# Low halves of the weights taken from PSUM, the last weight rows split a tile later, and twice as many table rows fetched by ScalarE

## The reference

```python
e = jnp.stack([tbl_f[ids[:, f]] for f in range(27)], axis=1)      # 2048 x 27 x 128, rows of 27 tables
gram = einsum('bfd,bgd->bfg', e, e)[:, upper triangle without diagonal]   # 351 products per example
h = concatenate([e.reshape(2048, 3456), gram, dense_ctx], axis=1)  # 3456 + 351 + 16 = 3823 columns
h = maximum(h @ W_top1 + b_top1, 0)      # 3823 x 512
h = maximum(h @ W_top2 + b_top2, 0)      # 512 x 256
y = h @ W_top3                           # 256 x 1
```

## Time and profile before

| | |
|---|---|
| median of 3 runs | 560.85 us (558.38 to 560.85) |
| the profiled execution | 560.3 us, of which 558.3 us are the span of the trace |
| busy in the span | PE 93%, PEld 88%, DVE 64%, ACT 42%, POOL 72% |
| chain of waits | PE 58%, POOL 27%, issue 9%, DMA 3% |
| gathers of GpSimd | 421, from 2.9 us to 531.0 us |

### The profile page before, as it was taken

One profiled execution on the slowest core, in us unless ns is written; L12 is line 12 of the kernel. 1 busy time (PEld: TensorE's weight loads), 2 busy tenths in 40 slices (PEclk: granted clock), 3 DMA queues, 4 the chain that ended last, 5 costly groups with the idle time before them and its releaser, 6 DMA issues.

```text
span 558.3 us, 10910 instructions
## 1 busy us (share of the span) xinstructions
PE 521.1 (93%) x2626; PEld 488.6 (88%) x2626; DVE 354.7 (64%) x1177; ACT 234.1 (42%) x721; POOL 404.4 (72%) x439
## 2 busy tenths in 40 slices
PE   0593899999999999999999999999999999999998
PEld 0483899999999999999999999999898998999985
DVE  2644675848476675847576575847567484766865
ACT  2643526254352625344252626345262533526251
POOL 6777777777777777777777777777777777777711
PEclk9988899999999999999999999999999999999999
DMA  8777221122111122121221212121211222121200
GB/s 183 231 212 206 56 55 53 54 57 57 55 55 55 54 60 55 54 56 53 58 57 55 55 55 55 56 58 54 55 54 55 58 55 56 53 55 54 56 11 1
DMA packets 26212, 38.05 MB, mean 68 GB/s; under 512 B 13156, under 2 KB 15588, under 8 KB 26148
## 3 DMA queue, kind: packets, MB, share of 16 engines
q0 software_dynamic: 13472, 27.62, 18.0%
q1 hardware_dynamic: 12164, 9.61, 6.5%
q10 hardware_dynamic: 512, 0.13, 0.1%
HBM read 37.31 MB, written 0.01 MB: 67 GB/s over the span
## 4 chain that ended last, share of the span: by engine, by line
PE 58%; POOL 27%; issue 9%; DMA 3%; DVE 1%; ACT 1%; SPq 0%; ACTq 0%; POOLq 0%; DVEq 0%
POOL emb L327 27%; PE ps_acc L387 14%; PE ps_acc L388 12%; PE ps_acc L389 11%; PE ps_gram L412 7%; PE ps_t L358 5%; PE ps_gram L505 2%; PE ps_acc L446 1%; DMA g_buf<-in_b_top 1%; PE ps_acc L447 1%; PE ps_acc L452 1%; PE ps_gram L498 1%; DMA emb<-in_tbl,idx_first 1%; PE ps_gram L441 1%; ACT g_buf L709 1%
## 5 line engine op out<-in xcount | busy, mean ns | idle before, releaser
L327 POOL DMA_INDIRECT emb<-in_tbl,idx x394 | 372.9, 946 | 120.2 <-issue 118.7
L387 PE MATMUL ps_acc<-w_hi,emb_x 128*128 128x512 f32 x432 | 197.3, 457 | 2.7 <-DVE emb_x L807 1.7
L388 PE MATMUL ps_acc<-w_lo,emb_x 128*128 128x512 f32 x432 | 175.3, 406 | 0.0
L847 DVE COPY g_buf<-ps_gram 32x112 f32<-32x112 f32 x480 | 129.8, 270 | 70.7 <-PE ps_gram L412 64.8
L389 PE MATMUL ps_acc<-w_hi,emb_x 128*128 128x512 f32 x432 | 174.4, 404 | 0.0
L644 ACT ACTIVATE emb_x<-ps_t 128x512 fp32r<-128x512 f32 (+1 forms) x111 | 63.5, 584 | 225.8 <-PE ps_t L358 206.5
L700 ACT ACTIVATE g_buf<-ps_gram 32x112 f32<-32x112 f32 x480 | 122.0, 254 | 56.9 <-PE ps_gram L412 51.2
L807 DVE TENSOR_TENSOR emb_x<-ps_t,emb_x 128x512 fp32r<-128x512 f32 (+1 forms) x111 | 72.8, 666 | 104.2 <-ACT emb_x L644 103.6
L387 PEld LDWEIGHTS ps_acc<-w_hi,emb_x 128*128 128x128 f32 x432 | 131.1, 304 | 8.6 <-issue 5.8
L388 PEld LDWEIGHTS ps_acc<-w_lo,emb_x 128*128 128x128 f32 x432 | 134.6, 312 | 0.8
L389 PEld LDWEIGHTS ps_acc<-w_hi,emb_x 128*128 128x128 f32 x432 | 131.9, 305 | 1.1
(11 more groups left out here) (81 smaller groups left out, 251.5 us busy)
## 6 DMA issues: line engine op xcount, KB each, us to landing
ahead<-in_tbl SPq DMA_DIRECT2D x1152, 0.5 KB
g_buf<-in_W_top SPq DMA_DIRECT2D x29, 256.0 KB, 3.6
emb<-in_tbl,idx POOLq DMA_INDIRECT x394, 2.5
beside<-in_tbl ACTq DMA_DIRECT2D x256, 0.5 KB
w<-in_W_top SPq DMA_DIRECT2D x1, 512.0 KB, 9.1
emb<-in_tbl,idx_first POOLq DMA_INDIRECT x27, 4.0
g_buf<-in_W_top SPq DMA_DIRECT2D x1, 222.0 KB
idx<-in_ids SPq DMA_DIRECT2D x1, 216.0 KB, 4.8
```

What stands on the lines that cost most here:

```text
L327: pool.indirect_dma_start(out=emb[:, f * D:(f + 1) * D], out_offset=None, in_=tables[f], in_offset=bass.IndirectOffsetOnAxis(ap=rows, axis ...
L387: pe.matmul(acc, emb_part(0, f), w_hi[:, f, :], start=(f == 0), stop=False)
L388: pe.matmul(acc, emb_part(0, f), w_lo[:, f, :], start=False, stop=False)
L847: last = dve.tensor_copy(target, source)
```

## The change

Three things:

1. **Low parts of weights.** ScalarE copies each chunk twice: to `w_hi`, and unrounded to a PSUM bank (`whole(c)`, the four gram banks in turn). VectorE's subtraction reads that bank in place of the stage buffer. The stage buffer is free when ScalarE's second copy is done (SyncE waits on `s_w_hi`).
2. **The last three chunks** are loaded into `h1`, `h1_t` and `gram` (buffers not yet in use) instead of stage buffers, with semaphores of their own. Both engines split them in tile 1, ScalarE ahead of its part on group 4, VectorE after packing the products of tile 0. The takes of tile 0 no longer wait for them.
3. **ScalarE fetches four sets of rows**: feature 22 of tiles 5, 8, 12 and 15. So GpSimd has 419 gathers. A tile's part is 38 rows. 22 addresses are loaded at group 4 and 16 more in the gram stage, between the takes of units 0 and 2. The row DMAs: 12 ahead of group 4, 3 ahead of group 5 and `take_columns`, 7 ahead of group 6, 1 each ahead of the takes of units 2, 4 and 8, 3 ahead of group 0 of the next tile (at unit 15), 2 ahead of its group 1 and 8 ahead of its group 2. The buffer `beside` keeps its size (two sets, used in turn).

The diff, cut to its core:

```diff
     BESIDE = 22
-    BESIDE_TILES = [8, 15]
+    BESIDE_TILES = [5, 8, 12, 15]
     NB = len(BESIDE_TILES)
-    A_SET = TILES // 2 - 1
-    A_TILE = 19
-    SLOTS = {4: (0, 11), 6: (11, 16), 2: (16, 19)}
-    assert BESIDE == AHEAD - 1 and A_SET * A_TILE >= P > A_SET * A_TILE - 8
+    A_TILE = 38
+    SLOTS = [("g", 4, 12), ("g", 5, 3), ("g", 6, 7), ("k", 2, 1), ("k", 4, 1), ("k", 8, 1), ("k", 15, 3), ("g", 1, 2), ("g", 2, 8)]
+    LOADS = [("g", 4, 22), ("k", 2, 16)]
+    assert sum(count for _, _, count in SLOTS) == sum(part for _, _, part in LOADS) == A_TILE
+    assert BESIDE == AHEAD - 1 and (TILES - 3) * A_TILE < NB * P <= (TILES - 2) * A_TILE
     HALF = H1 // 2
...
+        def whole(c):
+
+            return ps_gram[:, c % (BANKS + 1), :]
+
+        def cols_raw(n):
+
+            return (h1[:, :], h1_t[:, :], gram.rearrange("p a b -> p (a b)")[:, 0:H1])[n]
+
+        def cols_whole(n):
+
+            return ps_gram[:, BANKS - 1 + n % 2, :]
...
-                return beside[:, BESIDE_TILES.index(t), :]
+                return beside[:, BESIDE_TILES.index(t) % BESIDE_KEPT, :]
...
                 if c >= STAGES:
-                    sp.wait_ge(s_w_lo, c - STAGES + 1)
+                    sp.wait_ge(s_w_hi, c - STAGES + 1)
                 sp.dma_start(stage[:, s, :], w_top1[c * P:(c + 1) * P, :]).then_inc(s_w_raw[s], 16)
...
             for n in range(FULL):
-                load_weights(NF + n)
-            c = NF + FULL
-            sp.wait_ge(s_w_lo, c - STAGES + 1)
-            sp.dma_start(stage[0:REST - 1, c % STAGES, :], w_top1[c * P:K1, :]
-            sp.dma_start(stage[REST - 1:REST, c % STAGES, :],
+                sp.dma_start(cols_raw(n), w_top1[(NF + n) * P:(NF + n + 1) * P, :]
+                             ).then_inc(s_w_cols[n], 16)
+            sp.dma_start(cols_raw(FULL)[0:REST - 1, :], w_top1[(NF + FULL) * P:K1, :]
+                         ).then_inc(s_w_cols[FULL], 16)
+            sp.dma_start(cols_raw(FULL)[REST - 1:REST, :], b_top1.rearrange("(o n) -> o n", o=1)
+                         ).then_inc(s_w_cols[FULL], 16)
...
@@ -399,6 +415,7 @@
                     pe.wait_ge(s_emb_lo, NG * t + NG)
                     if t == 0:
                         pe.wait_ge(s_pads, 1)
+                        pe.wait_ge(s_w_lo, NF)
...
                     pe.wait_ge(s_ones, 2)
+                    pe.wait_ge(s_w_lo, NF + NCC)
...
         def _(act):
             def split_weights(c):
                 act.wait_ge(s_w_raw[c % STAGES], 16 * (c // STAGES + 1))
-                act.activation(w_hi[:, c, :], stage[:, c % STAGES, :],
+                act.activation(w_hi[:, c, :], stage[:, c % STAGES, :], ACT.Copy)
+                if c > BANKS:
+                    act.wait_ge(s_w_lo, c - BANKS)
+                act.activation(whole(c), stage[:, c % STAGES, :],
                                ACT.Copy).then_inc(s_w_hi, 1)
 
             def split_column_weights(n):
-                c, k = NF + n, COL_CHUNKS[n][1]
-                act.wait_ge(s_w_raw[c % STAGES], 16 * (c // STAGES + 1 + n // FULL))
-                act.activation(w_cols_hi[0:k, n, :], stage[0:k, c % STAGES, :],
+                k = COL_CHUNKS[n][1]
+                act.wait_ge(s_w_cols[n], 32 if n == FULL else 16)
+                act.activation(w_cols_hi[0:k, n, :], cols_raw(n)[0:k, :], ACT.Copy)
+                if n == 0:
+                    act.wait_ge(s_dve_raw, UNITS // 2)
+                if n >= 2:
+                    act.wait_ge(s_w_lo, NF + n - 1)
+                act.activation(cols_whole(n)[0:k, :], cols_raw(n)[0:k, :],
                                ACT.Copy).then_inc(s_w_hi, 1)
...
                 act.wait_ge(s_gram, UNITS * t + k + 1)
                 if k == 0:
                     if t == 0:
-                        act.wait_ge(s_w_lo, NF + NCC)
+                        act.wait_ge(s_w_lo, NF)
                     else:
                         act.wait_ge(s_turned, t)
...
+            def load_rows(rows, t, kind, number):
+
...
+                part = next(x for x in LOADS if x[0:2] == (kind, number))[2]
+                first = (t - 1) * A_TILE + len(rows)
+                end = min(first + part, NB * P)
+                while first < end:
+                    n, p = divmod(first, P)
+                    count = min(end - first, P - p)
+                    u = BESIDE_TILES[n]
+                    _, loaded = nc.values_load_multi_w_load_instructions(
+                        at_ahead[u:u + 1, P + p:P + p + count],
+                        engines=[mybir.EngineType.Activation],
+                        min_val=0, max_val=(tables[BESIDE].shape[0] - 1) * ROW,
+                        skip_runtime_bounds_check_because="an id is a row of its table")
+                    rows += [(n, p + i, at) for i, at in enumerate(loaded)]
+                    first += count
+
...
+            def fetch_beside(rows, kind, number):
+
+                slot = SLOTS.index(next(x for x in SLOTS if x[:2] == (kind, number)))
+                first = sum(count for _, _, count in SLOTS[:slot])
+                for n, p, at in rows[first:first + SLOTS[slot][2]]:
+                    if p == 0 and n >= BESIDE_KEPT:
+
+                        act.wait_ge(s_pe_t, NG * BESIDE_TILES[n - BESIDE_KEPT] + BESIDE // GF + 1)
+                    row = beside_bytes[bass.ds(at, ROW)]
+                    act.dma_start(beside[p:p + 1, n % BESIDE_KEPT, :].bitcast(u8),
                                   row.rearrange("(o b) -> o b", o=1)).then_inc(s_beside[n], 16)
...
+                    if t == 1 and g == 4:
+                        for n in range(NCC):
+                            split_column_weights(n)
                     if t > 0 and g == 4:
-                        picked = load_rows(t)
-                    if t > 0 and g in (4, 6) or t > 1 and g == 2:
-                        fetch_beside(picked, g)
+                        picked = []
+                        load_rows(picked, t, "g", 4)
+                    if t > 0 and g in (4, 5, 6) or t > 1 and g in (1, 2):
+                        fetch_beside(picked, "g", g)
                     if t > 0 and g == 5:
                         take_columns(t - 1)
...
-                if t == 0:
-                    for n in range(NCC):
-                        split_column_weights(n)
                 for k in ACT_UNITS:
+                    if t > 0 and k in (2, 4, 8, 15):
+                        if k == 2:
+                            load_rows(picked, t, "k", k)
+                        fetch_beside(picked, "k", k)
                     if k == UNITS - 1:
                         split_group(t + 1, 0)
                     take_blocks(t, k)
...
             def split_weights(c):
                 dve.wait_ge(s_w_hi, c + 1)
-                dve.tensor_tensor(w_lo[:, c, :], stage[:, c % STAGES, :],
+                dve.tensor_tensor(w_lo[:, c, :], whole(c),
                                   w_hi[:, c, :].bitcast(fp32),
                                   ALU.subtract).then_inc(s_w_lo, 1)
 
             def split_column_weights(n):
-                c, k = NF + n, COL_CHUNKS[n][1]
-                dve.wait_ge(s_w_hi, c + 1)
-                dve.tensor_tensor(w_cols_lo[0:k, n, :], stage[0:k, c % STAGES, :],
+                k = COL_CHUNKS[n][1]
+                dve.wait_ge(s_w_hi, NF + n + 1)
+                dve.tensor_tensor(w_cols_lo[0:k, n, :], cols_whole(n)[0:k, :],
                                   w_cols_hi[0:k, n, :].bitcast(fp32),
                                   ALU.subtract).then_inc(s_w_lo, 1)
...
                 dve.wait_ge(s_gram, UNITS * t + k + 1)
                 if t == 0 and k == 1:
-                    dve.wait_ge(s_w_lo, NF + NCC)
+                    dve.wait_ge(s_w_lo, NF)
...
                         if g == 3:
                             add_parts(t - 1)
                             pack_pairs(t - 1, 0, NF - 1)
+                            if t == 1:
+                                for n in range(NCC):
+                                    split_column_weights(n)
                             if t > 1:
                                 layer_3(t - 2)
-                if t == 0:
-                    for n in range(NCC):
-                        split_column_weights(n)
```

23 lines of the change are left out of this document (4 added, 19 removed).

## The result

| | before | after |
|---|---|---|
| median of the runs | 560.85 us (558.38 to 562.13) | 596.25 us (591.17 to 598.2, 4 runs) |
| the profiled execution | 560.3 us, span 558.3 | 598.2 us, span 596.1 |
| mean granted clock of its span | 0.985 | 0.963 |

The changed kernel is slower by a factor of 1.0623 (95% interval 1.0544 to 1.0701). The prediction had 588.8 us with a range of 574 to 607.

A forecast was written before the change was run, and what follows sets the result against it. TensorE's and GpSimd's paths were taken to end almost together. On TensorE's, 36.4 us of stops, less 5.1 at the start and 4.3 of gather waits, plus 1.5 for a clock fall gave +28.5 on 560.3: 588.8 us, range 574 to 607.

The forecast's parts named there:

- The direction and the mechanism: Slower (0.87): ScalarE's register loads delay its later copies and stop TensorE; loads starting at numbers not divisible by four are long.
- Rivals 2, 4 and 5: 2: flat register price, 610 us (0.05); 4: stops miss TensorE, faster (0.10); 5: only part of the stops, 562 (0.05).
- The sum of stops: TensorE's new stops from tile 1 to tile 14, behind ScalarE's loads and DMAs: 36.4 us together, bounds 32 and 40.
- Unit 5 in odd tiles: Gram stage: TensorE waits for unit 2's take behind the load, 3.15 us in odd tiles, about 0.7 in even ones.
- The stop ahead of the packed products in even tiles (L463): Longer load and more DMAs at groups 4 and 5 delay TensorE's first matmul on packed products by 1.3 us.
- tile 4: Its loads, split over two sets, stop TensorE 0.3 us at the packed products and 0.7 at unit 5.
- In tile 1: Late chunks' copies, load and row DMAs delay TensorE's first matmul on packed products: a stop of 3.95 us.
- one fall: TensorE's granted clock drops to the lower level once, after the stop in tile 1: 1.5 us added.
- rival 3: The clock falls after each stop of 3.15 us: six more falls, 1.5 to 3 us each, 598 to 607 (0.14).
- The start: TensorE's path in tile 0: 4.63 less stop, 1.0 later gram stage, 1.5 saved by clock; 5.1 us gained, bounds 3 and 7.
- The 4.63 us stop: Tile 0, unit 3: TensorE waits for takes held up by the last chunks; this stop was to go.
- GpSimd's path: Two gathers fewer (2.5 us) and undelayed start gathers (3.4): last gather issued 5.9 us earlier, vanishing in slack.

The follow-up runs named there:

- run 6: Changed kernel with 40 rows a tile in place of 38 and all 40 addresses loaded at group 4, none in the gram stage: 558.05 us, ratio 0.9932.
- the probes: Kernel before plus a register load and one row DMA between takes of units 0 and 2, tiles 1 to 14; four counts and starts: 567.24 to 625.0 us.
- run 5: Changed kernel with 40 rows a tile in place of 38, so every load starts at a number divisible by four: 565.03 us, ratio 1.0061.
- The first probe: Kernel before plus a load of 16 addresses from number 2 and one row DMA between takes of units 0 and 2: 625.0 us, ratio 1.1118.
- Part 1 alone: Kernel before with only the low parts taken from PSUM, ScalarE copying each of the first 27 chunks twice: 557.53 us, ratio 0.9922.
- the last run: Changed kernel, 44 rows a tile from tile 2 on, all addresses at group 4, SyncE's last set used in tile 15, not 14: 555.63 us, ratio 0.9905.
- parts 1 and 2: Changed kernel with rows fetched as before (two sets, 19 rows a tile): 557.15 us, ratio 0.9921.

## Why the prediction was right, and where it was off

- **The direction and the mechanism: right, and shown.** The load between the takes of units 0 and 2 stops TensorE at unit 5 (run 6 takes it away and the stops go), and the long loads are those whose first number is not divisible by four (the probes and run 5). The loads of the changed kernel came as worked out: 3.66 us in the gram stage of odd tiles and 1.21 in even ones, 1.89 and 4.94 at group 4. Rivals 2, 4 and 5 are out.
- **The sum of stops: 36.4 predicted, 31.2 measured.** Unit 5 in odd tiles 2.99 for 3.15, in even ones 0.55 for 0.7: the probes give a stop as the load less 0.65, and I had used less 0.5. The stop ahead of the packed products in even tiles (L463) was 0.65 to 1.07 for 1.3, and tile 4 had 0.82 in all for 1.0. In tile 1 3.30 for 3.95: the fifteen row DMAs ahead of `take_columns` took 3.93 + 0.82 = 4.75 us for the 5.4 that I had counted.
- **The clock: the mis-sized term.** I added one fall, 1.5 us. There were seven, worth 12.8 us. This is rival 3, to which I gave 0.14: six more falls of 1.5 to 3 us each, 598 to 607. They came at 1.5 to 2.7 us each, not all in the tiles that it names (none in tile 3, one in tile 7), and the smaller stops brought the time below 598. The step that failed is "I add one fall". The repeated stops of 3.15 us lay between a stop with a fall, 3.78, and one without, 1.71, and I counted them with the latter, though the former was the nearer row. The first probe shows 14 falls of 14 at 3.0 us. One trace was also too little to read a limit from: in six other profiles the same stop of 1.71 us has a fall behind it.
- **The start: 5.1 predicted, 4.3 measured**, within its bounds. The 4.63 us stop went. But the gram stage began 2.5 us later (49.23), not 1.0, and the clock gave back the rest: TensorE works about 4 us at half clock there, where it worked some 8.7 before. The delay stands in the timelines of SyncE and ScalarE of the changed kernel:

```profile
38.36 0.36 SPq L254 DMA_DIRECT2D g_buf<-in_W_top  x1
38.82 3.08 SPq L275 DMA_DIRECT2D ahead<-in_tbl  x3
41.95 0.37 SPq L254 DMA_DIRECT2D g_buf<-in_W_top  x1
42.42 0.88 SPq L275 DMA_DIRECT2D ahead<-in_tbl  x3
43.35 0.36 SPq L254 DMA_DIRECT2D g_buf<-in_W_top  x1
```
```profile
46.86 0.63 ACT L647 ACTIVATE w_hi<-g_buf 128x512 fp32r<-128x512 f32 x1 [0.86 <-DMA g_buf<-in_W_top]
```

  SyncE issues the last chunk of the main weights at 43.35 (before: 41.96). The three row fetches that take 3.08 us, a register load among them, are not the reason, as before has them too (3.12 us from 37.40). SyncE is late from chunk 14 on (21.88 for 20.46), since ScalarE needs about 1.04 us for the two copies of a chunk, and it stays so. ScalarE can split the last chunk only at 46.86, where the earlier trace rows have 44.81, and then comes the second copy.
- **GpSimd's path: right.** Part 1 alone brings the last gather 3.3 us forward for the 3.4 predicted, and in the last run, with both effects, it is issued at 525.1, 5.9 before the 531.0 of the earlier trace rows. In the changed kernel it came at 549.4, held back by TensorE's turns.
- **The total.** 37.9 us instead of 28.5: +11.3 by the clock (12.8 for 1.5), -5.2 by the stops, +0.8 by the start, +2.0 by the small losses in even tiles, which I had not counted. This sums to +8.9, and 0.5 stays open. Against the median of four runs, 596.25, the prediction was 7.5 us low. That this lies within the forecast's own 581 to 598 is in part luck: the clock alone would have brought 588.8 to 600.1, and the stops, 5.2 us too high, took half of it back.

## What to carry to other kernels

An instruction of a sequencer (a register load, a DMA issue) between two copies of one engine is a wait for whoever needs the second copy. Price it by the slack at that place, not by the engine's busy share: ScalarE was 42% busy. Put loads where the engine waits anyway, and give them starts that divide by four: 40 rows a tile and one place for the load turned a loss of 6.2% into a gain of 0.7%, though that gain is no more than what parts 1 and 2 have alone, 0.8%. And a stop of 3.0 us that recurred in each tile cost half as much again as its length, through TensorE's clock. Last, before shortening a start, look who sets the end: 5.7 us won on TensorE were worth nothing while GpSimd's gathers were in the lead.
